# Merge stage of a transformer layer: normalising moved from VectorE to GpSimd, a mask computed before a rank, and the first weight loads of the experts' networks held back

## The reference

```python
x = layernorm(x + attention(x))      # 16 heads, gated relative position bias, then @ Wo.T + bo
x = layernorm(x + ffn(x))            # 8 experts, two per token, with a capacity, and one fallback network
```

## Time and profile before

| stretch, us from the span's start | what runs there | PE busy | DVE busy | POOL busy | PE clock | GB/s |
|---|---|---|---|---|---|---|
| 2065.0 to 2109.3 | merge, up to the first `two_best` | 43.02 of 44.3 | 30.45 | 0.10 | 0.95 | 187 |
| 2109.3 to 2153.8 | part 0 is routed | 38.26 of 44.5 | 36.90 | 0 | 0.92 | 148 |
| 2153.8 to 2198.2 | part 1 | 38.15 of 44.4 | 36.89 | 0 | 0.92 | 192 |
| 2198.2 to 2238.7 | part 2 | 31.09 of 40.5 | 29.80 | 0 | 0.85 | 113 |
| 2238.7 to 2266.3 | part 3, routing alone | 9.33 of 27.6 | 15.70 | 0 | 0.50 | 6 |
| 2266.3 to 2277.1 | tile list, end of merge | 3.46 of 10.8 | 9.55 | 0 | 0.66 | 225 |
| 2277.1 to 2296.7 | ffn until its first rows | 0 of 19.6 | 11.74 | 9.30 | 0.50 | 255 |
| 2320 to 3275 | ffn | 951.40 of 955 | 384.86 | 611.47 | 1.00 | 211 |

### The profile page before, as it was taken

One profiled execution on the slowest core, in us unless ns is written; L12 is line 12 of the kernel. 1 busy time (PEld: TensorE's weight loads), 2 busy tenths in 40 slices (PEclk: granted clock), 3 DMA queues, 4 the chain that ended last, 5 costly groups with the idle time before them and its releaser, 6 DMA issues. The chain is left out here.

```text
span 3341.1 us, 58394 instructions
## 1 busy us (share of the span) xinstructions
PE 3099.0 (93%) x18893; PEld 2035.0 (61%) x18893; DVE 2384.1 (71%) x5688; ACT 2060.6 (62%) x4106; POOL 1522.6 (46%) x1916
## 2 busy tenths in 40 slices
PE   7986999999999999999999996875999999999991
PEld 4553555555555555554555553764888888888881
DVE  6877899989898899998999893775444443444436
ACT  3546999999999999998999993211322232232230
POOL 3444444444444444444444440003666666666650
PEclk9997999999999999999999998987999999999995
DMA  6883232333333232324232323534776667677666
GB/s 225 280 276 96 49 69 56 64 66 63 58 58 66 63 67 51 66 50 78 51 67 51 68 46 115 177 115 152 225 218 208 213 213 219 208 226 219 207 215 208
DMA packets 274612, 436.24 MB, mean 131 GB/s; under 512 B 58538, under 2 KB 202996, under 8 KB 255636
## 3 DMA queue, kind: packets, MB, share of 16 engines
q1 hardware_dynamic: 233108, 370.94, 39.9%
q0 software_dynamic: 30464, 44.94, 6.3%
q10 hardware_dynamic: 10752, 16.78, 1.3%
HBM read 325.60 MB, written 106.42 MB: 129 GB/s over the span
## 5 line engine op out<-in xcount | busy, mean ns | idle before, releaser
L837 DVE CUSTOM_DVE_ANT_0 tot<-sc,gbias 128x1024 f32<-128x1024 f32 x1024 | 1240.0, 1211 | 27.0 <-POOL gbias L698 26.7
L698 POOL TENSOR_SCALAR gbias<-slab_a,gs 128x484 f32<-128x484 f32 x1024 | 687.6, 673 | 867.4 <-DVE negm L837 847.1
L891 ACT ACTIVATE probs<-tot,negm 128x640 f32<-128x640 f32 (+2 forms) x1024 | 767.3, 749 | 41.6 <-DVE negm L837 33.5
L1465 ACT ACTIVATE f_hid<-f_ph,f_w_up 128x256 f32<-128x256 f32 (+1 forms) x584 | 268.5, 460 | 666.1 <-PE f_ph L1424 657.6
L740 PE MATMUL sc<-ks,qs 120*128 120x512 bf16 x2048 | 615.8, 382 | 38.5 <-PEq L207 22.4
L849 DVE COPY wt<-pb 128x256 f32<-128x256 f32 (+1 forms) x1024 | 398.1, 389 | 169.4 <-PE pb L761 168.9
L1424 PE MATMUL f_ph<-f_xt,f_w_up 128*128 128x256 f32 (+1 forms) x2336 | 484.6, 366 | 1.5 <-DVE f_xt L1484 1.2
L1436 PE MATMUL f_py<-f_w_down,f_hid 128*128 128x256 f32 x2176 | 481.6, 379 | 0.0
L916 ACT ACTIVATE wt<-pa 128x256 f32<-128x256 f32 (+1 forms) x1024 | 447.8, 437 | 43.2 <-PE pa L752 29.3
L752 PEld LDWEIGHTS pa<-ident,probs 128*128 128x128 f32 x2560 | 330.0, 140 | 227.8 <-issue 98.2
L1424 PEld LDWEIGHTS f_ph<-f_xt,f_w_up 128*128 128x128 f32 x2336 | 421.1, 191 | 55.6 <-issue 2.7
(11 more groups left out here) (203 smaller groups left out, 3171.3 us busy)
## 6 DMA issues: line engine op xcount, KB each, us to landing
f_w_down<-in_w_down SPq DMA_DIRECT2D x73, 1152.0 KB
f_w_up<-in_w_up SPq DMA_DIRECT2D x73, 1028.0 KB
ks<-k_d SPq DMA_DIRECT2D x192, 128.0 KB, 5.0
qs<-q_d SPq DMA_DIRECT2D x384, 64.0 KB
v_d<-vt SPq DMA_DIRECT2D x16, 1024.0 KB, 6.2
vs<-v_d SPq DMA_DIRECT2D x32, 512.0 KB, 6.8
rcb<-rc_d SPq DMA_DIRECT2D x64, 256.0 KB
q_d<-parts SPq DMA_DIRECT2D x32, 384.0 KB, 3.2
```

Of the source, the lines that this page charges most:

```text
L698: pool.tensor_scalar(gbias[x % NG][:, SIDE:SIDE + BAND], slab[:, hh, :], gs[u % 2][:, i, hh:hh + 1], 1.0, ALU.mult, ALU.mult).then_inc(gbi ...
L837: dve.tensor_tensor_reduce(tot[x % 2][:], sc[:, x % 2, :], gbias[x % NG][:, w:w + N], -1.0, 3.0e38, ALU.add, ALU.min, negm[h % 2][:, c:c + ...
L891: act.activation(probs[x % 2][:, 0:hi - lo], tot[x % 2][:, lo:hi], ACT.Exp, bias=negm[h % 2][:, c:c + 1], scale=-1.0).then_inc(near_done, 1)
```

## The change

In merge, DVE's `normalise` keeps only the reciprocal, now written to one of two buffers. POOL, which did nothing in this stage, runs a loop over the 16 chunks: it waits for `rstd_done` and normalises the four tiles. Before the first tile of a chunk is measured, DVE waits until POOL has finished the chunk before the last. In an expert's step the mask of kept tokens is computed first, with a semaphore of its own, then the rank, and then DVE waits for the mask's semaphore instead of the helper's. The instruction for `level2` moves from the tile list to slot 6 of the merge. In ffn, SP waits for the rows of tile 0 to have landed before it issues the second matrix of tile 0; whatever it issues after that, beginning with both matrices of tile 1, comes later as well.

```diff
-        rstd = sb("rstd", [P, TC])
+        rstd = sb("rstd", [P, 2, TC])
...
         def _(pool):
             pool.memset(eps[:], EPS).then_inc(eps_set, 1)
+            for c in range(NCH):
+                pool.wait_ge(rstd_done, c + 1)
+                for t in range(TC):
+                    pool.tensor_scalar(x1s[:, c * TC + t, 0:E], y[:, c % 2, t], mv[:, c % 2, t, 0:1], rstd[:, c % 2, t:t + 1],
+                                       ALU.subtract, ALU.mult).then_inc(x1_done, 1)
...
                 dve.wait_ge(counted, q * NETS + e + 1)
+                dve.scalar_tensor_tensor(out=kept[:, 0:k], in0=pp[:, 0:k], scalar=room[:, e:e + 1], in1=elig[:, 0:k], op0=ALU.is_lt, op1=ALU.mult).then_inc(kept_done, 1)
                 dve.scalar_tensor_tensor(out=rank[:, e, begin(q):ENDS[q]], in0=pp[:, 0:k], scalar=at[:, e:e + 1], in1=elig[:, 0:k], op0=ALU.add, op1=ALU.add)
-                then(dve.scalar_tensor_tensor(out=kept[:, 0:k], in0=pp[:, 0:k], scalar=room[:, e:e + 1], in1=elig[:, 0:k], op0=ALU.is_lt, op1=ALU.mult))
+                dve.wait_ge(kept_done, q * NE + e + 1)
                 then(dve.tensor_tensor(nfb[:, 0:k], rest[:, 0:k], kept[:, 0:k], ALU.add))
...
-                then(dve.tensor_scalar(level2[:], level[:], float(P), None, ALU.add))      # in tile_list
...
-            def normalise(c):
+            def invert_std(c):
                 dve.wait_ge(std_done, c + 1)
-                dve.reciprocal(rstd[:], std[:]).then_inc(rstd_done, 1)
-                dve.wait_ge(rstd_done, c + 1)
-                for t in range(TC):
-                    dve.tensor_scalar(x1s[:, c * TC + t, 0:E], y[:, c % 2, t], mv[:, c % 2, t, 0:1], rstd[:, t:t + 1], ALU.subtract, ALU.mult).then_inc(x1_done, 1)
+                dve.reciprocal(rstd[:, c % 2], std[:]).then_inc(rstd_done, 1)
 
             def measure(n):
                 c, t = n // TC, n % TC
+                if t == 0 and c >= 2:
+                    dve.wait_ge(x1_done, (c - 1) * TC)
...
                     then(dve.tensor_copy(x1s[:, :, E + 3], token[:]))                      # slot 6
+                    then(dve.tensor_scalar(level2[:], level[:], float(P), None, ALU.add))
...
                     sp.wait_ge(y_out, BEFORE[t - 1])                                       # ffn, SP, tile t
+                if t == 0:
+                    sp.wait_ge(x_in[0], landed(0, NX))
                 sp.dma_start(w_down[:, n], a["w_down"][bass.ds(net, 1)].rearrange("o p n -> p (o n)")).then_inc(down_in[n], 16)
```

More of the change, by code:

```diff
@@ L1012, in merge @@
             sem(n) for n in ("step", "shifted", "exped", "elig_done", "counted", "top_done", "slots_done"))
+        kept_done = sem("kept_done")
         capped_rank, spread, rank_turned, rank_copied, rank_stored, rows_stored = (
@@ L1308, in _ @@
                 if n >= 5 and (n - 5) % TC == 0 and (n - 5) // TC < NCH:
-                    normalise((n - 5) // TC)
+                    invert_std((n - 5) // TC)
                 if 1 <= n <= TT:
```

## The result

The changed kernel took 3366.15 us (median of 4 runs, 3359.52 to 3369.64) and the kernel before 3345.41 us (4 runs, 3342.19 to 3348.31, three of them those of the section before). The ratio is 1.006, 95% interval [1.004, 1.008]: 0.6% slower, where 0.24% faster was forecast. The profiled execution took 3359.52 us with a span of 3357.7 us, 16.6 us more than before.

The account below looks back on a forecast made before the run. PE was taken as ffn's bound (busy 951.4 of 955 us) and as pacing merge's routed slots. The terms -3.9 - 0.4 + 0.85 - 0.9 - 0.2 - 3.4 = -7.95 took 3342.88 to 3334.9 us, range 3331.0 to 3340.5.

Parts of the forecast that it names:

- Step 2: Merge: POOL's normalising instruction takes 0.48 us, priced from a same-shape row in ffn, and costs nothing in plain slots.
- rival A: Merge's plain slots: POOL becomes the bound, 0.93 us or more beside DVE instructions reading two SBUF tensors; slower, chance 0.06.
- The break-even: Merge's plain slots: score at T + 4.44, T being DVE's reciprocal start; PE held up only from 0.80 us an instruction.
- PE's clock: Merge's routed parts: PE's 5 us standstill during each two_best and its lower clock afterwards stay; no term in the sum.
- step 1: Merge's routed parts 0 to 2: relieving DVE shortens six long slots from 3.06 to 2.41 us, 3.9 us less.
- Step 3: Merge's first and last chunk: 0.4 us less in chunk 0, 0.85 us more in the last chunk.
- The sign that the prediction gave: Merge's last chunk: first score about 2.4 us after the end of its reciprocal, 0.8 later than now.
- Step 4: Merge's last part, 8 expert steps: mask before rank, 0.30 us from mask to next instruction, 0.9 us less.
- Step 5: Merge's tile list: moving level2 to slot 6 takes its instruction off the chain, 0.2 us less, possibly 0.
- Step 6: Start of ffn: delaying weights speeds tile 0's rank gather, first transpose 3.58 us earlier, 3.4 us less overall.
- Rival B: Start of ffn: the late weights give nothing, 3338.3 us in all, chance 0.22.

Follow-up runs that it names:

- e3: The kernel before with 96 probe instructions in eight forms on idle POOL in merge: mult and mult by 1.0 took 0.48 us, subtract and mult by pointers 1.23.
- e10: The kernel before with a second set of eight probe forms on POOL in merge: add and mult took 0.55 us, mult and subtract 1.23.
- e4: The changed kernel with POOL multiplying by the reciprocal and 1.0, leaving out the mean's subtraction: 3342.17 us, 0.9982 of the kernel before.
- e1: The changed kernel with ACT's store of a chunk issued behind the copies of its four tiles: 3341.74 us, 0.9981 of the kernel before.
- e5: The changed kernel with normalising written as mult and add, plus one small DVE instruction a chunk: 3340.03 us, 0.9982 of the kernel before.
- e6: e5 with ACT's store of a chunk issued behind the copies of its tiles, as in e1: 3337.89 us, 0.9975 of the kernel before.
- e8: e6 without ffn's late weights, so merge's edits alone: 3343.95 us, 0.9991 of the kernel before.
- e7: The kernel before with only ffn's late weights added: 3341.15 us, 0.9983 of the kernel before.
- e11: The kernel before profiled once more, unedited: two, one and one slow slots behind two_best, 8.13 us of clock excess; no whole time given.
- e2: The changed kernel with the four normalising instructions back on DVE: 3342.23 us, 0.9978 of the kernel before.
- e9: e6 with ten unread matmuls on PE ahead of the first count of parts 0 to 2: 3331.70 us, 0.9946 of the kernel before.

## Why the prediction was wrong

**Step 2 failed, by the price of POOL's instruction:** 0.48 us was taken, 1.22 measured. The row had the engine, the name `TENSOR_SCALAR` and the shape, but another pair of operations; the trace prints none, so the code should have been read beside the row. The forecast of 0.06 for rival A was too small for a price that no row showed, and the range ended at 3340.5 us, just short of the 3340.9 that the 0.93 us of the earlier trace rows give. The cause was not the one that rival A gave, a collision with DVE: e3 and e10 give at least 1.21 us for the form whatever DVE did beside it, all 64 instructions of after lie between 1.217 and 1.261 us, and e4 gives 0.48 in after's own place. As to the estimate of 0.55 us from the Trainium skill, GPSIMD Engine Reference, Performance versus the Vector engine: the page measured its 2.6 cycles an element on a `tensor_tensor` add of two inputs, which is another instruction. The estimate happens to fit the mult and add forms by pointer (0.55 and 0.56), and is off by a factor of 2.2 for subtract and mult (1.22).

**The break-even in the same step failed too: it was read from the wrong copy.** With the chunk's own score at T + 6.40 in place of T + 4.44, the prediction's working gives (5.6 - 0.39) / 4 = 1.30 us for a steady plain slot, and not 0.80. So 1.22 us costs nothing there, as the trace shows. At 1.22 us rival A's formula gives 32 x 0.42 + 4 x 0.74 - 7.95 = +8.5 us, thus 3351.3, the right direction for a wrong reason: the 32 x 0.42 charge slots that lost nothing. Without them it is -5.0 us, and the profiled execution took 16.6 us more. That loss is in chunk 0, around `places` and in the last chunk, where PE wants a chunk's first tile 3.4 to 5.3 us after the reciprocal; by the same working these places bear only about 0.6 to 1.0 us an instruction. But for the last chunk, the prediction did not look at them. What hands the price on to PE is the order on ACT's queue: the store, which needs all four tiles, stands ahead of a copy that needs one. Either the price or the order is enough to change: e1 keeps the price and has a rest of 164.2 us, e4 keeps the order and has 163.7, where after has 181.9.

**PE's clock was put at nothing in the sum.** That the lower clock behind each `two_best` would stay as it was, step 1 said without a reason. Against before it cost 9.6 us more in the slots behind `two_best`, and the clock was also lower behind each stall for POOL (0.83 and 0.91 where it had been 1.00). Of the +24.16 us of the stretch, 9.6 are clock excess; the other 14.6 are a gain of some 3.5 and a loss of some 18 (rest 181.9 against e4's 163.7). The excess also stays above before's where the stalls are gone. The profiles of e4, e5, e6 and e8 all have two, one and two slow slots, an excess of 10.6 to 11.4 us, where the unchanged merge has 6.2, 6.5 and 8.1 (before, e7, e11). Four profiles alike don't look like chance, and what in the change brings it is open. It takes back all that step 1 gains: the stretch of these four is -0.1 to +2.5 us against before's 173.48, where -3.45 was forecast.

**Step 1: the long slots went as said, the gain in time did not show.** In after no wait of PE for DVE's `incl` is left within parts 0 to 2 once they have started, and behind the slow slots counts are 2.41 us apart. The rest in e4, e5, e6 and e8 fell by 3.6, 1.9, 4.5 and 3.3 us, against 3.45 for steps 1 and 3 together. But the clock took it back, and by the timed runs the move to POOL is worth nothing that can be told from noise: e2 without it has 0.9978, e4 and e5 with it 0.9982, e6 0.9975, all with overlapping intervals.

**Step 3:** in after the gain in chunk 0 turned into a loss, with the price, and the loss in the last chunk grew. At 0.48 us the terms hold roughly. In chunk 0 of e4 PE waits 0.27 us for the first score in place of the 0.73 before, 0.46 less against 0.4. From the last chunk's reciprocal to `two_best` it takes 6.79 us before and 7.31 in e4, 0.52 more where 0.85 was taken, and 10.31 in after, 3.5 more where 0.85 + 4 x 0.74 is 3.8. With the store behind the copies (e6) it is 6.89. The sign that the prediction gave is misread: the first score of the last chunk already came 2.35 us after the reciprocal's end (2234.41 us, the reciprocal at 2231.88), and 0.8 more is 3.2.

**Step 4: right.** 0.30 us from mask to next instruction, as worked out; 1.04 us less in the last part against 0.9. It also shortens the long slots where DVE sets the pace (e2), where the prediction let PE cover it, which holds only as long as DVE doesn't normalise.

**Step 5:** +0.12 in after (10.88 us) and in e4, -0.21 in e6 (10.55) and -0.08 in e9 (10.68): at most 0.2, not settled.

**Step 6: right.** DVE's wait for the first ranks is 2.54 us in place of 6.27 (near 2.7 forecast), the first transpose 3.73 us earlier within the stage. Rival B is out by e7 and e8. Of the later loads only a little is seen: `up(0)` took 9.01 us in place of 8.65, at low clock.

The forecast's sum, -7.95 us, can be held against the kernels with a cheap form. e4, with the price that was taken, measured 0.18%, 6.0 us (3.3 to 9.0), and e6, which also has the later store, 0.25%, 8.4 us (4.7 to 12). That agreement is partly luck: the 4.4 us of excess that both profiles have more than before's were not in the sum, and step 6 gave more than it was put at (5.7 us, if not clear of 3.4). Profiles of single executions don't resolve this.

## What to carry to other kernels

Before an instruction is moved to another engine, find a row there with the same operations, not only the same name and shape; on GpSimd a subtract written as mult and add by a negated value cost half. When a producer becomes slower, look along the consumers' queues for an instruction that needs its last result and stands ahead of one that needs its first, and look at the chunks beside irregular work, not only at the steady ones. When a slack is read off a timeline, count the instructions from the stage's start, so that the copy and the score are those of the tile in question: here one slot's error, 1.96 us, put the break-even at 0.80 instead of 1.30 us. Where TensorE pauses for some 5 us and then is the bound, useless matmuls in the pause are worth a try: here they gave 10 us, more than the whole change was to bring.

## What the runs showed of the hardware that was not expected

- GpSimd's `tensor_scalar` on 128x256 float32 costs 0.40 us by two constants and 0.48 to 0.56 us with one or two pointers for pairs of mult and add, 0.93 us for a single operation, and 1.07 to 1.23 us for pairs with a subtract (e3 and e10, most of the twelve of each form). A single operation is dearer than a pair of mult and add.
- After a pause of TensorE of 5.04 to 6.02 us the granted clock was about 0.50 for one to three slots (4.2 to 14 us) in all profiles but one, though TensorE was busy all through them (9.20 of 9.20 us in after); how many differs from execution to execution. With 4.56 us of matmuls in the pause the first two slots took 2.40 to 2.44 us, all three times.
- POOL and DVE did get in each other's way, if not enough to matter in after. Beside the probes of e10 four normalising instructions of DVE take up to 1.76 us in place of 1.38, single small instructions with two SBUF inputs up to 0.40 in place of 0.18 (`m_r_nfb`), and single slots grow from 3.06 to 3.98 us (e10's third of part 0), while the add from PSUM (median 418 ns in both) and the statistics (427 and 428) don't change. The Trainium skill, GPSIMD Engine Reference, Specifications, says that GpSimd and VectorE contend where VectorE's instruction has two SBUF inputs or runs in a two-port mode. The unchanged add and statistics and the longer small instructions agree with it; in which mode the normalising instructions run, no run here shows.
